# Rotary by pairs of heads over neighbouring PSUM banks, score masks added by VectorE and softmax sums taken by ScalarE, in a transformer block on one core

## What is computed

```python
h = tokens(x) + pos_embedding                      # 592 x 256
n = layernorm(h)
q, k, v = n @ Wq, n @ Wk, n @ Wv                   # 8 query heads, 4 key and value heads, 128 wide
q, k = (y * cos + rotate_half(y) * sin for y in (q, k))
s = q @ k.T / sqrt(128), masked above the diagonal
h = h + (softmax(s) @ v) @ Wo
n = layernorm(h)
h = h + shared experts(n) + sum over the top 4 of 16 of gate * expert(n)
```

## Time and profile before

| | |
|---|---|
| median of 3 runs | 159.1 us |
| the profiled execution | 159.16 us |
| its span, first to last instruction | 157.2 us |
| outside of the span | 1.96 us |
| PE busy | 150.4 us, 96% |
| VectorE (DVE) busy | 125.3 us, 80% |
| ScalarE (ACT) busy | 95.5 us, 61% |
| GpSimd (POOL) busy | 63.6 us, 40% |

### The profile page before, as it was taken

One profiled execution on the slowest core, in us unless ns is written; L12 is line 12 of the kernel. 1 busy time (PEld: TensorE's weight loads), 2 busy tenths in 40 slices (PEclk: granted clock), 3 DMA queues, 4 the chain that ended last, 5 costly groups with the idle time before them and its releaser, 6 DMA issues.

```text
span 157.2 us, 3252 instructions
## 1 busy us (share of the span) xinstructions
PE 150.4 (96%) x1101; PEld 140.9 (90%) x1101; DVE 125.3 (80%) x336; ACT 95.5 (61%) x230; POOL 63.6 (40%) x62
## 2 busy tenths in 40 slices
PE   6999979999999999999999999999999999999990
PEld 2888669888999997999989999999999999999990
DVE  0035987879899999999894756889996897969993
ACT  0305878899667885976184299687446646575220
POOL 0005997556458573293910000139243542630300
PEclk9999999999999999999999999999999999999998
DMA  5999900000000007992000000000000000000004
GB/s 153 324 378 363 383 12 4 2 2 4 0 0 0 4 0 255 425 422 105 2 0 4 0 2 0 0 0 4 0 6 0 0 0 4 0 0 0 0 4 154
DMA packets 5745, 11.86 MB, mean 75 GB/s; under 512 B 914, under 2 KB 3682, under 8 KB 5602
## 3 DMA queue, kind: packets, MB, share of 16 engines
q1 hardware_dynamic: 4434, 9.91, 17.2%
q10 hardware_dynamic: 1296, 1.75, 3.1%
HBM read 11.05 MB, written 0.61 MB: 74 GB/s over the span
## 4 chain that ended last, share of the span: by engine, by line
PE 83%; DVE 12%; issue 2%; ACT 1%; DVEq 0%
PE bank L1070 62%; PE bank L1085 6%; PE bank L1162 4%; PE bank L1189 4%; DVE h L830 2%; PE bank L1078 2%; PE bank L1174 2%; DVE qk L718 1%; PE bank L1158 1%; PE bank L1213 1%; DVE stats L679 1%; DVE hn L701 1%; DVE qk L725 1%; DVE ssum L753 1%; PE bank L1114 1%
## 5 line engine op out<-in xcount | busy, mean ns | idle before, releaser
L393 POOL TENSOR_TENSOR exp_lo<-ffn_sb,exp_hi 128x512 fp32r<-128x512 f32 x18 | 24.3, 1355 | 49.3 <-ACT exp_hi L510 48.3
L830 DVE SCALAR_TENSOR_TENSOR h<-bank,gate,h 128x256 f32<-128x256 f32 (+1 forms) x80 | 32.5, 473 | 1.1 <-PE bank L1070 1.0
L1070 PE MATMUL bank<-exp_hi,act_hi 128*128 128x256 f32 (+1 forms) x90 | 25.4, 282 | 0.0
L1070 PE MATMUL bank<-exp_lo,act_hi 128*128 128x256 f32 (+1 forms) x90 | 25.3, 281 | 0.0
L1070 PE MATMUL bank<-exp_hi,act_lo 128*128 128x256 f32 (+1 forms) x90 | 25.2, 280 | 0.0
L377 POOL TENSOR_TENSOR swapped<-swapped,sin_sb 128x296 f32<-128x296 f32 x24 | 20.0, 837 | 12.5 <-ACT swapped L482 12.2
L810 DVE TENSOR_TENSOR act_lo<-act,act_hi 128x256 fp32r<-128x256 f32 (+1 forms) x36 | 18.4, 527 | 5.6 <-ACT act_hi L522 4.9
L519 ACT ACTIVATE act<-bank 128x256 f32<-128x256 f32 (+1 forms) x36 | 15.3, 424 | 11.8 <-PE bank L1070 11.4
L1070 PE MATMUL bank<-hnT_hi,exp_hi 128*128 128x256 f32 (+1 forms) x72 | 21.9, 304 | 0.0
L1070 PE MATMUL bank<-hnT_hi,exp_lo 128*128 128x256 f32 (+1 forms) x72 | 21.5, 299 | 0.0
L1070 PE MATMUL bank<-hnT_lo,exp_hi 128*128 128x256 f32 (+1 forms) x72 | 21.5, 298 | 0.0
(11 more groups left out here) (96 smaller groups left out, 369.9 us busy)
## 6 DMA issues: line engine op xcount, KB each, us to landing
ffn_sb<-w_ffn SPq DMA_DIRECT2D x6, 768.0 KB, 7.9
wqkv_sb<-w_qkv SPq DMA_DIRECT2D x4, 512.0 KB, 8.6
wo_sb<-w_o SPq DMA_DIRECT2D x1, 1024.0 KB, 11.0
x_sb<-xT ACTq DMA_DIRECT2D x3, 192.0 KB, 4.9
x_sb<-xT SPq DMA_DIRECT2D x3, 192.0 KB, 4.8
out<-h SPq DMA_DIRECT2D x2, 256.0 KB, 2.2
wp_sb<-wpT SPq DMA_DIRECT2D x3, 128.0 KB, 4.4
wp_sb<-wpT ACTq DMA_DIRECT2D x3, 128.0 KB, 5.1
```

The lines of the kernel that those rows point to most:

```text
L393: nc.gpsimd.tensor_tensor(exp_lo[:, e % SPLIT_RING, :], ffn_sb[:, e, :], exp_hi[:, e % SPLIT_RING, :].bitcast(F32), ALU.subtract).then_inc ...
L830: last = nc.vector.scalar_tensor_tensor(h[r, i, :], y, gate[r, i, one], h[r, i, :], ALU.mult, ALU.add)
L1070: last = nc.tensor.matmul(ps, a, b, start=(n == 0 and m == 0), stop=(n == len(pairs) - 1 and m == 2 and not more))
```

## The change

The rotary stage works on two heads at once, in 12 steps in place of 24. Banks 4 and 5, and 6 and 7, become two tensors of two neighbouring banks; a unit takes one of them, and `swap`, `sine`, `cosine` and `rope_add` are each one instruction (or pair of them) over 2 x 296 columns. Both halves of the tokens use both pairs of banks. The turned probabilities of groups 0 and 1 go to banks 0 and 1, so `turn_probs(0, .)` now waits until all values are kept (`v_kept`), and the first `project` calls wait for `h_kept`.

The mask matmul and the two casts are gone. VectorE takes, for each head, one `tensor_tensor_reduce`: it adds the mask to the scores, scales by -1/sqrt(128), writes that, and gives the row's minimum. ScalarE takes, for each head, one exponential with scale -1 and that minimum as its bias per row, and gives the row's sum. So a quad has four instructions of each where it had two on VectorE and one on ScalarE, and VectorE's row sums are gone. Five `aux` tiles share memory with the tiles that are needed early.

All engines' lists are in a new order. Cut to its core:

```diff
-        ROPE_ORDER = [0, 8, 1, 2, 9, 3, 4, 10, 5, 6, 11, 7]
+        ROPE_ORDER = [(0, 8), (1, 2), (3, 9), (4, 10), (5, 6), (7, 11)]
-            return bank[(0, 1, 6, 7, 0)[i]]
+            return bank[(0, 1, 6, 5, 0)[i]]
+        def rope_banks(n):
+            return bank_pair[(n + 1) % 2]
+        def turned_probs(g, c):
+            return c if g < 2 else 6 + c
...
             def sine(n):
-                nc.gpsimd.tensor_tensor(swapped[:, n % 3, :], swapped[:, n % 3, :], sin_sb[:],
-                                        ALU.mult).then_inc(qk_sin, 1)
+                nc.gpsimd.tensor_tensor(swapped[:, n % 3], swapped[:, n % 3],
+                                        sin_sb[:].unsqueeze(1).broadcast_to([P, 2, HT]), ALU.mult).then_inc(qk_sin, 1)
...
             def swap(n):
-                ps = bank[rope_bank(n)]
-                nc.scalar.activation(swapped[0:64, n % 3, :], ps[64:128, 0:HT], ACT.Copy)
-                nc.scalar.activation(swapped[64:128, n % 3, :], ps[0:64, 0:HT], ACT.Copy).then_inc(qk_swapped, 1)
+                ps = rope_banks(n)
+                nc.scalar.activation(swapped[0:64, n % 3], ps[64:128, :, 0:HT], ACT.Copy)
+                nc.scalar.activation(swapped[64:128, n % 3], ps[0:64, :, 0:HT], ACT.Copy).then_inc(qk_swapped, 1)
...
             def exps(g, c):
-                nc.scalar.activation(quad(probs, g, c), quad(probs, g, c), ACT.Exp, scale=SCALE).then_inc(sc_exp, 1)
+                for j in range(QUAD):
+                    hd = QUAD * c + j
+                    scores_of = probs[0:GN[g], g % 2, hd, 0:GN[g]]
+                    last = nc.scalar.activation(scores_of, scores_of, ACT.Exp, bias=slow[0:GN[g], g, hd:hd + 1], scale=-1.0,
+                                                accum_out=ssum[0:GN[g], g, hd:hd + 1])
+                last.then_inc(sc_exp, 1)
...
             def cosine(n):
-                nc.vector.tensor_tensor(qk[:, head, half(b)], bank[rope_bank(n)][:, 0:HT], cos_sb[:],
-                                        ALU.mult).then_inc(qk_cos, 1)
+                nc.vector.tensor_tensor(pair_of(qk, n), rope_banks(n)[:, :, 0:HT],
+                                        cos_sb[:].unsqueeze(1).broadcast_to([P, 2, HT]), ALU.mult).then_inc(qk_cos, 1)
             def rope_add(n):
+                nc.vector.tensor_tensor(pair_of(qk, n), pair_of(qk, n), swapped[:, n % 3], ALU.add).then_inc(qk_roped, 1)
...
             def less_max(g, c):
-                nc.vector.tensor_reduce(smax[0:GN[g], g, QUAD * c:QUAD * c + QUAD], quad_bank(2 + c, g),
-                                        AX_X, ALU.max).then_inc(sc_max, 1)
-                nc.vector.tensor_tensor(quad(probs, g, c), quad_bank(2 + c, g), per_head(smax, g, c),
-                                        ALU.subtract).then_inc(sc_less, 1)
+                for j in range(QUAD):
+                    hd = QUAD * c + j
+                    last = nc.vector.tensor_tensor_reduce(
+                        probs[0:GN[g], g % 2, hd, 0:GN[g]], bank[2 + c][0:GN[g], j * GN[g]:(j + 1) * GN[g]],
+                        mask_f[0:GN[g], 0:GN[g]], -SCALE, -MASKED, ALU.add, ALU.min, slow[0:GN[g], g, hd:hd + 1])
+                last.then_inc(sc_less, 1)
             def inv_sum(g, c):
-                nc.vector.tensor_reduce(ssum[0:GN[g], g, QUAD * c:QUAD * c + QUAD], quad(probs, g, c),
-                                        AX_X, ALU.add).then_inc(sc_sum, 1)
...
             def project(n):
+                if n >= 2:
+                    pe.wait_ge(qk_cos, n - 1)
+                else:
+                    pe.wait_ge(h_kept, 3 + n)
+                for j, head in enumerate(heads):
...
             def scores(g, c):
-                nc.tensor.matmul(quad_bank(2 + c, g), ident_b[0:GN[g], 0:GN[g]],
-                                 mask_b[0:GN[g], :, 0:GN[g]], start=True, stop=False, skip_group_check=True)
...
             def turn_probs(g, c):
                 pe.wait_ge(sc_norm, 2 * g + c + 1)
+                if g == 0:
+                    pe.wait_ge(v_kept, NG)
+                elif g == 1:
+                    pe.wait_ge(pv_lo_kept, c + 1)
```

More of the change, by code:

```diff
@@ L879, in _ @@
             norm_apply(3)
+            norm_stats(4)
             norm_apply(4)
             cosine(0)
-            constants(0)
+            cosine(1)
             rope_add(0)
-            for n in range(1, 4):
-                cosine(n)
-            turned_low(3)
-            rope_add(1)
-            constants(1)
-            rope_add(2)
-            rope_add(3)
+            wo_low()
+            cosine(2)
+            turned_low(3)
+            turned_low(4)
+            cosine(3)
+            for n in range(1, 4):
+                rope_add(n)
@@ L891, in _ @@
             cosine(4)
             cosine(5)
-            turned_low(4)
             rope_add(4)
             rope_add(5)
-            for n in range(6, 9):
-                cosine(n)
-            for n in range(6, 9):
-                rope_add(n)
-            wo_low()
+            cosine(6)
+            less_max(0, 0)
+            less_max(0, 1)
+            rope_add(6)
+            less_max(1, 0)
+            cosine(7)
+            cosine(8)
+            inv_sum(0, 0)
+            rope_add(7)
@@ L901, in _ @@
+            less_max(1, 1)
+            inv_sum(0, 1)
+            inv_sum(1, 0)
+            rope_add(8)
+            inv_sum(1, 1)
             cosine(9)
-            less_max(0, 0)
+            less_max(2, 0)
+            rope_add(9)
             cosine(10)
-            cosine(11)
-            for n in range(9, 12):
-                rope_add(n)
-            inv_sum(0, 0)
-            cosine(12)
-            less_max(0, 1)
-            rope_add(12)
-            cosine(13)
-            cosine(14)
@@ L933, in _ @@
-            cosine(20)
-            cosine(21)
-            less_max(3, 0)
-            rope_add(20)
-            rope_add(21)
             heads_low(0, 0)
             heads_low(0, 1)
-            cosine(22)
-            cosine(23)
-            rope_add(22)
-            rope_add(23)
+            rope_add(10)
+            cosine(11)
+            less_max(2, 1)
+            rope_add(11)
+            inv_sum(2, 0)
+            less_max(3, 0)
+            inv_sum(2, 1)
+            less_max(3, 1)
@@ L959, in _ @@
+            inv_sum(5, 0)
+            add_residual(1)
+            norm_stats(6)
+            turned_low(5)
             heads_low(3, 0)
             heads_low(3, 1)
-            turned_low(5)
-            inv_sum(4, 0)
-            inv_sum(4, 1)
-            inv_sum(5, 0)
+            less_max(5, 1)
+            norm_apply(6)
             inv_sum(5, 1)
-            add_residual(1)
-            norm_stats(6)
+            heads_low(4, 0)
             add_residual(2)
             norm_stats(7)
-            norm_apply(6)
+            turned_low(6)
@@ L971, in _ @@
             norm_apply(7)
-            heads_low(4, 0)
             heads_low(4, 1)
-            turned_low(6)
             turned_low(7)
@@ L1118, in project @@
             def project(n):
[L1119 to L1120 removed]
+                b, heads = rope_unit(n)
+                if n % PAIRS == 0:
                     pe.wait_ge(lo_made, tiles_with((b + 1) * HT))
[L1122 to L1133 removed]
+                if n >= 2:
[3 more added lines that the diff above has]
+                for j, head in enumerate(heads):
+                    if n < PAIRS:
+                        pe.wait_ge(qkv_lo_made, QKV_ORDER.index(head * D // CHUNK) + 1)
+                    cs = slice(head * D, (head + 1) * D)
+                    last = three(rope_banks(n)[:, j, 0:HT],
+                                 [(wqkv_hi[:, k, cs], wqkv_lo[:, k, cs], hnT_hi[:, k, half(b)], hnT_lo[:, k, half(b)])
+                                  for k in range(KH)])
+                last.then_inc(qk_made, 1)
             def values(g):
```

398 lines of the change are left out of this document (162 added, 236 removed).

## The result

The changed kernel has a median of 157.4 us over 5 runs (157.14 to 158.15), the kernel before 159.1 us (158.94 to 159.25) on the same chip: ratio 0.9906, 95% interval 0.9888 to 0.9925. So it is 1.5 us faster (1.2 to 1.8), where 3.5 us slower was forecast. In two later comparisons the same kernel gave 0.9921 and 0.9906. The profiled execution took 157.14 us, span 155.4. The nearest of the figures named ahead is rival A's, 157.0; how far A's mechanism held is said in the part on the prediction.

A forecast was written before the change was run, and what follows sets the result against it. PE was taken to bound the kernel throughout. Exponentials add 17.2 us to ScalarE, swaps save 4.0; ScalarE saturates, moving the fourth output projection from 83.4 to 86.9: 159.16 + 3.5 = 162.7 us, range 157.1 to 167.3.

The forecast's parts named there:

- rival A: ScalarE's row sums nearly free, quad 0.8 to 1.4 us (limit about 1.6), PE stays bound: 157.0 us; chance 0.22.
- ScalarE, exponentials: Softmax on ScalarE: 0.50 us a head, 2.0 us a quad of 111; 23.5 us in place of 6.3.
- the gate: Fourth tile's output projection, gated by ScalarE's heads_high(4, 1), starts at 86.9 us where before it was 83.4.
- ScalarE has no slack, each 0.1 us on the quad is 1.2 us of time: ScalarE full from 42 to 86 us; each 0.1 us on the quad moves the end by 1.2 us.
- over 19 of 20: Sign that the forecast is right: ScalarE busy over 19 of 20 us in any stretch from 44 to 84 us.
- PE loses 2.0 us: Mask matmuls gone from PE: 2.0 us less, all on the path as long as PE bounds the stage.
- VectorE's saving is worth nothing by itself: VectorE loses some 10 us of its 57 but is no bound, so no time is gained.
- VectorE's sizes: VectorE: cosine 0.77 us, softmax head of 111 275 ns, rope_add at most what it was; some 10 us less.
- Case C: VectorE's tensor_tensor_reduce is two instructions, 8.6 us come back; with quads of 2.4 us, 167; chance 0.08.
- The start: norm_stats(4) behind two turned_low on VectorE: first projection 0.4 us earlier, 20.7 in place of 21.1.
- Swaps: Rotary half swaps on ScalarE over 592 columns: 0.66 us each, 4.0 us less in all.
- experts and what follows them unchanged: After the fourth output projection nothing is added; the experts stay PE's 54.3 us.

The follow-up runs named there:

- e8: Changed kernel without row sums, the reciprocal reading the row minima instead: 156.56 us, ratio 0.9846.
- e1: Changed kernel with one more one-column copy on ScalarE behind each exponential: 161.63 us, ratio 1.0156.
- e4: Kernel before without its mask matmuls, the mask left out of what is computed: 158.36 us, ratio 0.9951.
- e2: Changed kernel with a bf16 matmul of zeros of the mask's size in each quad, overwritten by the scores: 158.54 us, ratio 0.9968.
- e7: Changed kernel with the row sums back on VectorE and none with ScalarE's exponentials: 159.96 us, ratio 1.0062.
- e3: Kernel before with only norm_stats(4) moved behind norm_apply(3) on VectorE, as the change has it: 159.97 us, ratio 1.0059.
- e11: Changed kernel with qkv_high(3) on ScalarE back ahead of turned_high(1) and (2): 158.63 us, ratio 0.9974.
- e10: Kernel before with only qkv_high(3) on ScalarE moved behind turned_high(1) and (2): 159.69 us, ratio 1.0035.
- e14: Changed kernel itself, measured again in a later comparison: 157.87 us, ratio 0.9921.
- e13: Changed kernel with attend(4, 1), heads_high(4, 1), heads_low(4, 1) ahead of the third output projection, turn_norm(7) behind attend(5, 1): 158.23 us, ratio 0.9952.
- e16: Changed kernel itself once more, in another later comparison: 157.56 us, ratio 0.9906.
- e5: Changed kernel, in its own order, with the mask matmul and softmax of the kernel before: 162.83 us, ratio 1.0254.

## Why the prediction was wrong, point by point

- **ScalarE, exponentials: the step that failed**, as a size. "I let bias and half of that overlap cancel and take 296 + 203 = 0.50 us a head." The bias costs 378 - 296 = 82 ns (52 taken) and the read 190 ns (203 taken). That the 82 ns are the bias's and not the sum's shows e8, whose exponentials without a sum take 378 ns too. But the overlap of 0.1 us in the earlier trace rows is there between all eight instructions of a quad, twice a head, where I granted half of one: 378 + 190 - 2 x 98 = 0.37 us. The twelve quads take 8 x 1.5 + 4 x 1.36 = 17.4 us and not 23.5; of the 6.1 us between, 5.0 are the difference of the gate (81.9 in place of 86.9). The Trainium skill, ScalarE: Activation LUTs, section What ACT_TABLE_LOAD costs, gave 93 ns both for the overlap and for the operand per partition, and the trace agrees (98 and 82 ns). I had weighed it and gone by a mean between it and nothing, for one pair of rows was all I had; the safer choice was to apply an overlap that was seen to every neighbour of its kind. Not to every neighbour on the engine: the two halves of a swap take 0.66 us each and start 0.67 us apart (55.30 and 55.97 us), with no overlap.
- **ScalarE has no slack, each 0.1 us on the quad is 1.2 us of time**: right above 1.5 us (e1: 4.0 us for 0.37), wrong below (e8: at most 1.0 for 0.29). ScalarE is busy 19.04 of 20 us from 46 to 66 us, and over 19 of 20 I had named as a sign of the forecast; it was no such sign, for an engine can be nearly full and in time.
- **PE loses 2.0 us, all on the path while PE bounds**: of these 2.0 us only 0.7 (e4) to 1.0 (e2) come through. What the earlier trace rows show as PE without gaps has VectorE right behind it in the kernel before, and ScalarE in the changed one (e8).
- **"VectorE's saving is worth nothing by itself"**: by itself it was not tried, but within the change it is worth a lot. With the sums on VectorE the changed order is 2.5 us slower (e7), and in the kernel before it holds back most of the mask's gain, by its busy time and PE's waits (e4). It was at 19.36 of 20 us in the second stretch, and I read only its whole.
- **VectorE's sizes**: `cosine` 0.77 as measured; the head 0.20 us and not 0.275; `rope_add` 1029 ns, and not at most two of before. In sum 7.7 us less over the span (8.3 less in the three stretches of the earlier trace rows), not some 10.
- **Case C**: its form came true (two instructions), its price not: the read lies beside the next head's main instruction. The Trainium skill, VectorE: DVE Perf Modes, section Two Vector instructions with no wait between them, had the form.
- **The start**: 0.4 us was about right, but by luck, for the cause was wrong. The first projection comes at 20.6 us on average of eleven profiled kernels with the changed start (20.16 to 21.17), and at 21.0 on average of three with the start of before (20.89 to 21.11). `norm_stats(4)` gives nothing by itself (e3); `qkv_high(3)` behind `turned_high(2)` does, 0.7 to 0.8 us in the changed order (e11), and it costs 0.6 in the other (e10). Part of what makes the same kernel's start vary by 1 us is in the traces. In the changed kernel and in e14 the chain before the first projection begins with the DMA of the first weight piece: ScalarE's `qkv_high(0)` starts at 12.81 and 13.81 us, and the first projection follows 7.35 and 7.36 us later. In e13 and e16 it runs through PE's matmuls of the tokens instead. Why either comes late was not settled.
- **Swaps** 662 ns, experts and what follows them unchanged: right.
- **Rival A**: its figure came close, its mechanism only in part. PE does stay nearly without waits, and the quad of 1.5 us is below A's limit of 1.6. But the sums are not free: the quad is above A's own 0.8 to 1.4, and the mask gives 0.7 to 1.0 us where A kept all of its 2.0. That 157.0 fits so well is partly luck.
- **Sum of what was found**: middle 0.7, end 0.15, start 0.4 to 0.8 make 1.3 to 1.7 us, against 1.5 measured. How much of the middle's 0.7 us the new order of the lists gave by itself was not measured. No run beat the changed kernel with the whole computation in it.

## What to carry to other kernels

Price a run of short instructions by the distance of their starts, not by the sum of their durations: where one pair in the trace overlaps, take that for every pair of the same kind, and let the other value be the rival. When work moves from one engine to another and both are nearly full, find the knee, the price per step at which the receiver stops fitting, and ask on which side of it each plausible price falls; here 0.13 us a head decided the sign. And a relief is worth what the stretch says in which it falls: an engine at 19 of 20 us there is the next bound behind the one that you relieve, whatever its share of the span.

## What was not expected of the hardware

- A row sum on ScalarE is an instruction of 190 ns of which 0.1 us shows; a row minimum on VectorE is one of 82 ns of which nothing shows (heads 0.20 us apart with a main part of 269 ns).
- `rope_add` over 592 columns, both inputs in SBUF, takes 1029 ns on average, single ones between 0.77 us (at 46.09, 56.06) and 1.52 us (at 47.91, beside GpSimd's multiplications), against 772 ns for `cosine` of the same size out of banks. What makes one long is in the order of the starts (start us, us):

```profile
41.29 1.47 POOL L378 TENSOR_TENSOR swapped<-swapped,sin_sb 128x592 f32<-128x592 f32 x1 [0.17 <-ACT swapped L476]
42.37 1.03 DVE L713 TENSOR_TENSOR qk<-qk,swapped 128x592 f32<-128x592 f32 x1
46.09 0.77 DVE L713 TENSOR_TENSOR qk<-qk,swapped 128x592 f32<-128x592 f32 x1
46.32 1.32 POOL L384 TENSOR_TENSOR probs<-probs,sinv 111x444 f32<-111x444 f32 x1
```

A long `rope_add` starts while a GpSimd multiplication runs, and it ends 0.63 or 0.64 us behind that one's end: 43.40 against 42.76 us here, 43.70 against 43.07 and 47.55 against 46.92 in e1. The one at 46.09 starts with GpSimd's row from 44.75 all but done (46.22) and takes 0.77 us, and then GpSimd's next is the long one: 1.32 us at 46.32 against 0.93 at 50.58, where no `rope_add` runs beside it. In these rows the two engines hold each other up, and the later to start pays.

- After PE's wait of 1.7 us in e7, with PE busy 2.32 of 4 us, the granted clock averaged 0.64 over the next 4 us: between the levels of 1.2 and 2.4 GHz, mostly at the lower one. Eight attend matmuls took 2.99 us where the changed kernel needs 1.58 at full clock. So this wait of PE costs more than its own length. The same is seen in e5, where PE is busy 2.01 of 4 us from 56 us on and the clock is 0.68 over the next 4. In e1 PE is busy 3.01 of 4 us from 48 us on, and the clock stays at 1.00. The changed kernel's clock was 1.00 in the same stretches.
